# Cross-attention with a routed expert layer: scores of two heads at a time, one pair of banks ahead of the exponentials

## The chip, the cores and the metric

One NeuronCore of a Trainium2 chip runs the whole program in one launch. The metric is the device time of that launch in microseconds. The engines meant below are PE (TensorE), ACT (ScalarE), DVE (VectorE), POOL (GpSimd) and SP (SyncE, which here only issues DMAs).

## The reference

Eight batches of 112 tokens of width 512 attend to 375 context tokens each (257 image tokens and 118 text tokens, each part with its own key and value weights and its own softmax), with 16 heads of 32. Then each token goes through two of eight experts.

```python
x = x + xattn(layernorm(x), ctx)           # 8 x 112 x 512, ctx 8 x 375 x 512
#   q = rms_norm(x @ Wq.T + bq) * w ; k, k_img likewise from ctx_txt, ctx_img ; v, v_img linear
#   out = softmax(q k_img / sqrt(32)) v_img + softmax(q k / sqrt(32)) v   per head ; out @ Wo.T + bo
x = x + moe(layernorm(x))                  # gate softmax, top 2 of 8 experts,
#   expert: gelu(x W1 + b1) -> gelu(. W2 + b2) -> . W3 + b3
```

## The kernel before

All is float32 in and out. Products that need it are made of three fp32r products of high and low parts (high x high, high x low, low x high): the high part is a rounding copy on ACT, the low part a subtraction on DVE.

**Bodies and slots.** The attention part is a software pipeline written out in full: `body(b, p)` for b from -1 to 8 on each engine, each body with 16 slots `h`, one per head. In body b the heads of batch b are computed, the projections of batch b + 1 are prepared (`has_prep`, bodies -1 to 6), and the rest of batch b - 1 is done (`has_tail`: output projection, second LayerNorm, gate). Every engine goes through its own list in order, and the lists meet at semaphores, so the place of an instruction in its engine's list is the schedule.

**PE.** In slot h: every fourth slot (h = 0, 4, 8, 12) the scores of a group of four heads (`score`, L1042: 12 matmuls with 32 rows each, heads in different row groups, into the four PSUM banks of `scores`); then the transposes of the probabilities of head h - 2 (`transpose`, L1051, into `ptb`, `LAG` is 2); in slots 2, 6, 10, 14 the product with the values (`attend`, L1068 and L1072, into `pvb`); and a piece of projection work, the `FILL` of the slot: v2 in slots 0 and 1, k0 in 2, o (the output projection) in 3 and 4, xT in 4, k1 in 5, qt in 6 and 7, k2 in 8, q and kt in 9, kt in 10, kx and k3 in 11, v0 and ms in 12, v0 and rb in 13, v1 in 14 and 15. They use two PSUM banks (`tiles`) in turn, which ACT or DVE empties (`stage`).

**Softmax.** DVE's `maxima` (L753, L754) takes the negated maxima of two heads at a time for the image and the text part; ACT's `weigh` (L543, L545) makes the exponentials of one head with their sums, `take_transposed` (L553) copies the transposed probabilities. For a group of four heads, DVE's `invert_sums` (L761) writes reciprocals of the sums, each repeated 32 times, into `rx`; PE transposes them behind `attend`, ACT copies them (`take_sums`, L559), DVE multiplies (`attended`, L766, L768), and the result is split (L563, L772). DVE did both `maxima` of a group at the head of slots 0, 4, 8, 12; ACT did `weigh` ahead of `take_transposed` in the slots between, and at the end of those four slots.

**RMS norm.** The squares of q and k are written by ACT (`sq`: L499, L510, L519). DVE adds the four chunks (L833 in slot 11, L788 and L790 in slot 12), PE sums over partitions (`ms`, L1017), DVE scales (L736), POOL takes the power -0.5 (L442), PE spreads it (`rb`, L1021), ACT copies it (L516), and DVE multiplies queries and keys (L722, L700, L701). Then come the high and low parts of the next body's queries and first key chunk (L533, L526 on ACT, L747, L743 on DVE) in slot 14. The other key chunks are split in the slots of `KEYS_HIGH_AT` and `KEYS_LOW_AT`. ACT adds the bias to the image keys (L511) just behind their square.

**Context.** `cr` holds the raw context of a batch, loaded by SP (L308); ACT copies its image part in slot 0 and its text part in slot 2 (L280, `ch_done`), DVE subtracts in slots 1 and 3 (L672, `cl_done`). SP waits for both before the load of the next, and behind that load stand the load of x (L310), the store of `x1` (L334, after the bank of o is read), the store of `xn2` (L344) and the load of `xr` (L351). The last body's SP list begins with three loads of expert weights.

**After the attention** come routing on DVE and PE, the scatter by indirect DMAs, and a loop over blocks of 256 tokens with the expert weights (from about 460 us to the end); the change does not touch it.

Of the kernel before, what the change touches and what calls it, by code (L numbers as in the profile page):

```python
# [23 lines left out]
P = 128  # L24
# [38 lines left out]
KEYS_LOW_AT = {2: 1, 6: 2, 10: 3}  # L63
# [29 lines left out]
def cross_attention_moe(nc, x, ctxT, ctx_last, wT, vecs, o_b, wg, bg, experts, b12, b3, out):  # L93
    with ExitStack() as ctx:
# [41 lines left out]
        rx = sb("rx", [P, 2, 4, HD])  # L136
# [14 lines left out]
        for i in (1, 0):  # L151
# [87 lines left out]
            "x_in", "c_in", "ch_done", "cl_done", "xr_in", "xr_ob", "ln1_stats", "ln1_mv", "ln1_var", "ln1_rstd", "xn_done",  # L239
            "ln2_stats", "ln2_mv", "ln2_var", "ln2_rstd", "xh_done",  # L240
            "squares", "sum_a", "sum_b", "r_done", "rms_done", "q_done", "k_done", "qh_done", "ql_done", "kh_done", "kl_done", "rows_stored", "rows_in",
            "s_ready", "max_done", "exp_done", "rsum_done", "t_ready", "pt_done",
# [33 lines left out]
        def split_ctx(act, n, i):  # L276


            act.wait_ge(S["c_in"], 16 * n)
            act.activation(c_part(cH)[i], cr[:, :, PARTS[i]], ACT.Copy).then_inc(S["ch_done"], 1)  # L280

        @block.sync
        def _(sp):
# [12 lines left out]

            def body(b, p):
                if has_heads(b):

                    if b > 1:  # L300
                        sp.wait_ge(S["pv_ready"], NC * (b - 1))
                    sp.dma_start(vx[0:1, p, :], vlast_d[b:b + 1, :]).then_inc(vrow_in[p], 16)
                if has_prep(b):

                    if b < LAST - 1:
                        sp.wait_ge(S["ch_done"], 2 * (b + 2))
                        sp.wait_ge(S["cl_done"], 2 * (b + 2))
                        sp.dma_start(cr, ctxT[b + 2]).then_inc(S["c_in"], 16)  # L308
                        sp.wait_ge(S["xn_done"], b + 2)
                        sp.dma_start(xb[0:L, :], x[b + 2]).then_inc(S["x_in"], 16)  # L310
                if fixed(b, -1):

                    sp.wait_ge(S["zeroed"], 1)
                    by_partition = slots_d.rearrange("(p r) d -> p r d", p=P)
                    for r in range(0, ROWS, B):
                        n = min(B, ROWS - r)
                        sp.dma_start(by_partition[:, r:r + n, :], xr[:, :].unsqueeze(1).to_broadcast([P, n, D])).then_inc(S["zero_stored"], 16)

                    sp.wait_ge(S["vlast_sb"], 1)
                    sp.dma_start(vlast_d, vlast).then_inc(S["vlast_out"], 16)  # L320
                    sp.wait_ge(S["vlast_out"], 16)
                    sp.wait_ge(S["cleared"], 1)
                if fixed(b, LAST):


                    sp.wait_ge(S["pv_ready"], NC * LAST)
                    sp.wait_ge(S["cl_done"], 2 * B)
                    sp.wait_ge(S["k_done"], NC * B)
                    for pc in range(3):
                        sp.dma_start(raw[pc], experts[0, pc]).then_inc(raw_in[pc], 16)  # L330
                if has_tail(b):

                    taken(sp, "o", b)
                    sp.dma_start(x1_d[b - 1], x1[0:L, :]).then_inc(S["x1_stored"], 16)  # L334
                    if fixed(b, DONE):
# [78 lines left out]
        def _(pool):  # L414
# [55 lines left out]
        def _(act):  # L470
# [11 lines left out]
            def stage(name, b, p):  # L482
# [13 lines left out]
                if name == "q":  # L496

                    taken(act, "q", b)
                    act.activation(sq[:, :, 0:L], qn[:, 1 - p, :, :], ACT.Square).then_inc(S["squares"], 1)  # L499
# [5 lines left out]
                if name in ("k0", "k1", "k2", "k3"):  # L505

                    act.wait_ge(tile_ready[bank], cnt + 1)
                    c = int(name[1])
                    bias = vec[:, V_KIB, c:c + 1]
                    act.activation(sq[:, c, L:L + IMG], tiles[:, bank, 0:IMG], ACT.Square, bias=bias).then_inc(S["squares"], 1)  # L510
                    act.activation(kn[1 - p][:, c, 0:IMG], tiles[:, bank, 0:IMG], ACT.Identity, bias=bias).then_inc(tile_free[bank], 1)  # L511
# [5 lines left out]
                if name == "kx":  # L517
                    taken(act, "kx", b)
                    act.activation(sq[:, :, L + IMG:TOK], kn[1 - p][:, :, IMG:KEYS], ACT.Square).then_inc(S["squares"], 1)  # L519

            def split_keys(b, p, c):

                act.wait_ge(S["k_done"], NC * b + c + 1)
                if not (fixed(b, 0) and c < 2):
                    act.wait_ge(S["s_ready"], NC * b + c - 1)
                act.activation(kH[:, c % 2, :], kn[p][:, c, :], ACT.Copy).then_inc(S["kh_done"], 1)  # L526

            def split_queries(b, p):

                act.wait_ge(S["q_done"], b + 1)  # L530
                if not fixed(b, 0):
                    act.wait_ge(S["s_ready"], NC * b)
                act.activation(qH, qn[:, p, :, :], ACT.Copy).then_inc(S["qh_done"], 1)  # L533
# [36 lines left out]
            def body(b, p):  # L570
                for h in range(NH):
# [4 lines left out]
                    if h == 14 and has_prep(b):  # L576
                        split_queries(b + 1, 1 - p)
                        split_keys(b + 1, 1 - p, 0)
# [19 lines left out]
                    if h == 0 and has_prep(b) and not fixed(b, -1):  # L598
                        split_ctx(act, b + 2, 0)
                    for name in STAGE_AT[h]:  # L600
                        if has(name, b):
                            stage(name, b, p)
                    if h % 4 == 0 and has_heads(b):
                        weigh(b, p, h)
                    if h == 2 and has_prep(b) and not fixed(b, -1):
                        split_ctx(act, b + 2, 1)
# [48 lines left out]
        def _(dve):  # L655
# [14 lines left out]
            def split_ctx_low(n, i):  # L670
                dve.wait_ge(S["ch_done"], 2 * n - 1 + i)
# [77 lines left out]
            def maxima(b, g, i):  # L749

                dve.wait_ge(S["s_ready"], NC * b + g + 1)
# [4 lines left out]
            def invert_sums(b, g):  # L756
# [4 lines left out]
                dve.reciprocal(rx[0:L], sums[0:L, g % 2, :, :].unsqueeze(3).to_broadcast([L, 2, 4, HD])).then_inc(S["rsum_done"], 1)  # L761
# [16 lines left out]
            def body(b, p):  # L778
                for h in range(NH):
# [11 lines left out]
                    if h % 4 == 0 and has_heads(b):  # L791
                        maxima(b, h // 4, 0)
                        maxima(b, h // 4, 1)
# [16 lines left out]
                    if h in (1, 3) and has_prep(b) and not fixed(b, -1):  # L810
                        split_ctx_low(b + 2, h // 2)
# [35 lines left out]
                    if h == 0 and fixed(b, FIRST):  # L847
                        dve.wait_ge(S["small_in"], 64)

# [107 lines left out]
        def _(pe):  # L957
# [74 lines left out]
            def score(b, p, g):  # L1032
# [42 lines left out]
            def body(b, p):  # L1075
# [4 lines left out]
                for h in range(NH):  # L1080
                    if h % 4 == 0 and has_heads(b):
                        score(b, p, h // 4)
# [161 lines left out]
```

## Time and profile before

| | us |
|---|---|
| median of 3 runs | 931.02 (930.43 to 933.33) |
| the profiled execution | 931.23 |
| its span | 929.4 |
| attention bodies 1 to 6, each | 46.47 |

| engine | busy us | share of the span |
|---|---|---|
| PE (matmul) | 773.7 | 83% |
| PE (weight load) | 676.3 | 73% |
| DVE | 588.3 | 63% |
| ACT | 505.8 | 54% |
| POOL | 69.6 | 7% |

The shares are means over stages with different limits: set-up until 47 us, the attention bodies until about 415 us, routing and scatter until about 460 us, and then the experts. The ends of matmuls are modelled, so a busy PE is not one at its peak, and a gap between two matmuls is a little longer than the idle time that the profile gives. The time from one event to another is best taken start to start.

### The profile page before, as it was taken

How to read it: one execution, taken by the hardware profiler on the slowest of the kernel's cores; microseconds unless marked ns; L12 is line 12 of the kernel's file. 1: busy time of each engine (PE TensorE's matmuls, PEld its weight loads, DVE VectorE, ACT ScalarE, POOL GpSimd, SP SyncE). 2: the span in 40 equal slices, each digit the busy share in tenths (PEclk: the TensorE clock that was granted, in tenths of full speed). 3: DMA queues.
4: the chain of work that ended last, by engine and by line, in shares of the span. 5: the costliest groups of instructions: out<-in, count | busy, mean ns of one | idle time of the engine just before them, and what ended most of it. 6: DMA issues, size and time to landing. Idle time of an engine off the chain costs nothing.

```text
span 929.4 us, 17429 instructions
## 1 busy us (share of the span) xinstructions
PE 773.7 (83%) x6238; PEld 676.3 (73%) x6238; DVE 588.3 (63%) x1001; ACT 505.8 (54%) x1154; POOL 69.6 (7%) x94
## 2 busy tenths in 40 slices
PE   2888989898989898773079999999999999999930
PEld 2566666666666666552079999999999999999920
DVE  5466767676767676746136767676767676767634
ACT  4566767676767676751044545454545555555510
POOL 2100000000000000000600000000000000000014
PEclk9989999999999999855579999999999999999975
DMA  7850102010202000407625656565656565656568
GB/s 245 312 210 1 64 11 64 12 64 11 63 12 65 11 22 11 158 11 260 204 86 187 233 184 236 185 235 183 236 184 236 184 236 184 234 183 237 181 226 259
DMA packets 33982, 137.53 MB, mean 148 GB/s; under 512 B 3712, under 2 KB 3728, under 8 KB 22928
## 3 DMA queue, kind: packets, MB, share of 16 engines
q1 hardware_dynamic: 31200, 129.23, 40.0%
q0 software_dynamic: 2736, 7.69, 2.9%
q8 instruction: 28, 0.46, 0.2%
q14 instruction: 18, 0.15, 0.0%
HBM read 115.36 MB, written 21.54 MB: 147 GB/s over the span
## 4 chain that ended last, share of the span: by engine, by line
PE 68%; DVE 9%; ACT 9%; issue 7%; DMA 3%; POOL 2%; SPq 0%; POOLq 0%; ACTq 0%; DVEq 0%
PE tiles L960 7%; PE tiles L962 7%; PE tiles L961 7%; PE scores L1191 4%; PE scores L1193 4%; PE scores L1192 4%; PE ptb L1051 3%; PE pvb L962 3%; PE pvb L961 3%; PE pvb L960 3%; PE ptb L962 3%; PE ptb L961 3%; PE ptb L960 3%; PE scores L1042 2%; ACT scr L543 2%
## 5 line engine op out<-in xcount | busy, mean ns | idle before, releaser
L776 DVE TENSOR_TENSOR w<-scr,w 128x2048 fp32r<-128x2048 f32 x76 | 174.2, 2292 | 84.6 <-ACT w L568 84.6
L568 ACT ACTIVATE w<-scr 128x2048 fp32r<-128x2048 f32 x76 | 144.8, 1907 | 63.2 <-PE scores L1193 59.3
L960 PE MATMUL tiles<-c,w 128*128 128x256 f32 (+1 forms) x272 | 83.0, 305 | 22.1 <-DVE c L672 17.5
L1051 PE MATMUL ptb<-ident,scr 112*128 112x112 f32 x384 | 64.4, 279 | 25.9 <-ACT scr L553 25.9
L960 PE MATMUL tiles<-w 128*128 128x256 f32 x288 | 81.5, 283 | 0.0
L961 PE MATMUL tiles<-w 128*128 128x256 f32 x288 | 81.5, 283 | 0.0
L962 PE MATMUL tiles<-w 128*128 128x256 f32 x288 | 81.5, 283 | 0.0
L961 PE MATMUL tiles<-c,w 128*128 128x256 f32 (+1 forms) x272 | 79.9, 294 | 0.0
L962 PE MATMUL tiles<-c,w 128*128 128x256 f32 (+1 forms) x272 | 79.9, 294 | 0.0
L1051 PEld LDWEIGHTS ptb<-ident,scr 112*128 112x128 f32 x384 | 44.1, 149 | 48.9 <-ACT scr L545 35.1
L553 ACT ACTIVATE scr<-ptb 128x336 f32<-128x336 f32 x128 | 59.9, 468 | 26.9 <-PE ptb L1051 26.9
L960 PEld LDWEIGHTS tiles<-c,w 128*128 128x128 f32 x272 | 55.0, 202 | 25.4 <-issue 21.8
L543 ACT ACTIVATE scr<-scores,nmax 112x257 f32<-112x257 f32 x128 | 62.6, 489 | 12.7 <-DVE nmax L754 12.7
L933 DVE CAST w<-scr 128x256 fp32r<-128x256 f32 x144 | 41.6, 289 | 43.7 <-ACT scr L642 42.7
L935 DVE TENSOR_TENSOR w<-scr,w 128x256 fp32r<-128x256 f32 x144 | 61.2, 425 | 5.1 <-DVE w L933 0.2
L642 ACT ACTIVATE scr<-tiles,b12s 128x256 f32<-128x256 f32 x72 | 33.2, 473 | 56.9 <-PE tiles L962 56.8
L1191 PE MATMUL scores<-w 128*128 128x512 f32 x144 | 57.0, 396 | 0.0
L1193 PE MATMUL scores<-w 128*128 128x512 f32 x144 | 56.2, 390 | 0.0
L1192 PE MATMUL scores<-w 128*128 128x512 f32 x144 | 56.0, 389 | 0.0
L761 DVE RECIPROCAL rx<-sums 112x256 f32<-112x256 f32 x32 | 55.7, 1741 | 0.0
L961 PEld LDWEIGHTS tiles<-c,w 128*128 128x128 f32 x272 | 55.2, 203 | 0.4
L960 PEld LDWEIGHTS tiles<-w 128*128 128x128 f32 x288 | 55.3, 192 | 0.0
(212 smaller groups left out, 2120.9 us busy)
## 6 DMA issues: line engine op xcount, KB each, us to landing
scr<-in_dram SPq DMA_DIRECT2D x86, 1024.0 KB, 4.8
slots_d<-xr SPq DMA_DIRECT2D x3, 2048.0 KB, 17.5
scr<-in_dram SPq DMA_DIRECT2D x8, 750.0 KB, 4.9
scr<-slots_d SPq DMA_DIRECT2D x10, 512.0 KB, 4.6
slots_d<-scr SPq DMA_DIRECT2D x9, 512.0 KB, 3.8
xn<-in_dram SPq DMA_DIRECT2D x10, 256.0 KB, 4.7
xb<-in_dram SPq DMA_DIRECT2D x8, 224.0 KB, 4.9
xr<-in_dram SPq DMA_DIRECT2D x8, 224.0 KB, 2.5
```

The lines of the kernel that those rows point to most:

```text
L543: act.activation(probs[0:L, s, 0:IMG], scores[0:L, s, 0:IMG], ACT.Exp, bias=nmax[0:L, g, s, 0:1], accum_out=sums[0:L, g, 0, s:s + 1])
L553: act.activation(probT[:, h % 8, :, :], ptb[:, 0:KT * L].rearrange("p (t q) -> p t q", t=KT), ACT.Copy).then_inc(S["pt_done"], 1)
L568: act.activation(EH[slot], raw[slot], ACT.Copy).then_inc(S["eh_done"], 1)
L776: dve.tensor_tensor(EL[slot], raw[slot], EH[slot].bitcast(F32), ALU.subtract).then_inc(S["el_done"], 1)
L935: dve.tensor_tensor(hL[lay][:, c, :], gel[:, m % 4, :], hH[lay][:, c, :].bitcast(F32), ALU.subtract).then_inc(S["hl_done"], 1)
L960: pe.matmul(out, wh, xh, start=start, stop=False)
L961: pe.matmul(out, wh, xl, start=False, stop=False)
L962: return pe.matmul(out, wl, xh, start=False, stop=stop)
L1051: mm = pe.transpose(ptb[:, t * L:(t + 1) * L], probs[0:L, h % 4, t * P:(t + 1) * P], ident[0:L, 0:L])
L1191: pe.matmul(yb[:, t, :], h_hi, wh[:, i, :], start=(f == 0), stop=False)
L1192: pe.matmul(yb[:, t, :], h_hi, wl[:, i, :], start=False, stop=False)
L1193: mm = pe.matmul(yb[:, t, :], h_lo, wh[:, i, :], start=False, stop=(f == 7))
```

## The change

PE computes the scores of two heads at a time: `score(b, j)` for the pair j (heads 2j and 2j + 1), in two of the four banks, in the odd slots 2j - 1 behind the transposes; the first pair of a body is computed at the end of slot 15 of the body before. It waits for the exponentials of the heads up to 2j - 3, which the transposes ahead of it have waited for already. DVE takes the maxima of pair j at the end of slot 2j - 1 (pair 0 at the head of slot 0), and ACT's `weigh` stands ahead of `take_transposed` in every slot but slot 0, where it stands behind the split of the context; the splits for the next body's queries and first keys stand behind both in slot 14. `invert_sums` takes the reciprocals of the eight sums and then copies them 32-fold. All squares are made on POOL, from the keys and queries with their bias, and so is the copy of the text part of the context. The x1 store stands ahead of the context load on SP. Key chunk 3's low part moves from slot 10 to slot 9.

```diff
-KEYS_LOW_AT = {2: 1, 6: 2, 10: 3}
+KEYS_LOW_AT = {2: 1, 6: 2, 9: 3}
...
+            def next_context(b):
+                sp.wait_ge(S["ch0_done"], b + 2)
+                sp.wait_ge(S["ch1_done"], b + 2)
+                sp.wait_ge(S["cl_done"], 2 * (b + 2))
+                sp.dma_start(cr, ctxT[b + 2]).then_inc(S["c_in"], 16)
...
                     sp.dma_start(x1_d[b - 1], x1[0:L, :]).then_inc(S["x1_stored"], 16)
+                if FIRST <= b < LAST - 1:
+                    next_context(b)
...
+            def square(name, b, p):
+
+                taken(pool, name, b)
+                if name == "q":
+                    to, of = sq[:, :, 0:L], qn[:, 1 - p, :, :]
+                elif name == "kx":
+                    to, of = sq[:, :, L + IMG:TOK], kn[1 - p][:, :, IMG:KEYS]
+                else:
+                    c = int(name[1])
+                    to, of = sq[:, c, L:L + IMG], kn[1 - p][:, c, 0:IMG]
+                pool.tensor_tensor(to, of, of, ALU.mult).then_inc(S["squares"], 1)
...
                     rstd(b + 2, mv1, ve1, rs1, "ln1")
+                    if not fixed(b, -1):
+                        pool.wait_ge(S["c_in"], 16 * (b + 2))
+                        taken(pool, "v2", b)
+                        pool.tensor_copy(c_part(cH)[1], cr[:, :, PARTS[1]]).then_inc(S["ch1_done"], 1)
+                    if not fixed(b, -1):
+                        pool.wait_ge(tile_ready[tile_use("ms", b - 1)[0]], tile_use("ms", b - 1)[1] + 1)
+                    square("k0", b, p)
                 if has_tail(b):
                     rstd(b, mv2, ve2, rs2, "ln2")
                 if has_prep(b):
+                    for name in ("k1", "k2", "q", "kx", "k3"):
+                        square(name, b, p)
...
                     if fixed(b, -1) and h in WEIGHTS_AT:
                         split_weights(WEIGHTS_AT[h])
-                    if h % 4 and has_heads(b):
+                    if h and has_heads(b):
                         weigh(b, p, h)
                     if h < LAG:
                         if has_tail(b):
                             take_transposed(b - 1, NH - LAG + h)
                     elif has_heads(b):
                         take_transposed(b, h - LAG)
+                    if h == 14 and has_prep(b):
+                        split_queries(b + 1, 1 - p)
+                        split_keys(b + 1, 1 - p, 0)
...
-                dve.reciprocal(rx[0:L], sums[0:L, g % 2, :, :].unsqueeze(3).to_broadcast([L, 2, 4, HD])).then_inc(S["rsum_done"], 1)
+                dve.reciprocal(rsum[0:L], sums[0:L, g % 2, :, :]).then_inc(S["inverted"], 1)
+                dve.wait_ge(S["inverted"], NC * b + g + 1)
+                dve.tensor_copy(rx[0:L], rsum[0:L].unsqueeze(3).to_broadcast([L, 2, 4, HD])).then_inc(S["rsum_done"], 1)
...
+                    if h % 2 and h < NH - 1 and has_heads(b):
+                        maxima(b, (h + 1) // 2)
...
-                if not (fixed(b, 0) and g == 0):
-
-                    pe.wait_ge(S["exp_done"], NH * b + 4 * g)
+                if not (fixed(b, 0) and j < 2):
+
+                    pe.wait_ge(S["exp_done"], NH * b + 2 * j - 2)
                 for n, (q, k) in enumerate(((qH, kH), (qH, kL), (qL, kH))):
-                    for i in range(4):
+                    for i in (2 * j % 4, 2 * j % 4 + 1):
...
-                    if h % 4 == 0 and has_heads(b):
-                        score(b, p, h // 4)
...
+                    if h % 2 and h < NH - 1 and has_heads(b):
+                        score(b, (h + 1) // 2)
...
+                    if h == NH - 1 and has_prep(b):
+                        score(b + 1, 0)
```

## Rows read from the trace of the kernel before

**Rows 1.** The page: busy times, the chain that ended last, the context loads.

```profile
PE 773.7 (83%) x6238; PEld 676.3 (73%) x6238; DVE 588.3 (63%) x1001; ACT 505.8 (54%) x1154; POOL 69.6 (7%) x94
...
PE 68%; DVE 9%; ACT 9%; issue 7%; DMA 3%; POOL 2%; SPq 0%; POOLq 0%; ACTq 0%; DVEq 0%
...
scr<-in_dram SPq DMA_DIRECT2D x8, 750.0 KB, 4.9
```

**Rows 2.** Windows: stretch, its length, each engine's busy time, TensorE's clock, DMA.

```profile
185.47:231.94 46.47, 41.00 (x389) 31.92 (x388) 32.54 (x67) 33.09 (x113) 3.72 (x6) 1.00 0.12 38
...
387.60:412.00 24.40, 16.57 (x154) 12.27 (x154) 11.79 (x20) 12.46 (x48) 1.26 (x1) 0.50 0.07 20
```

**Rows 3.** TensorE's waits from 95 to 395 us: total us, times, longest.

```profile
PE ptb L1051 <- ACT scr L553: 20.5, 27, 1.9
PE tiles L1021 <- ACT scr L495: 4.1, 6, 0.7
PE scores L1042 <- ACT scr L545: 3.8, 6, 0.6
PE tiles L980 <- ACT xn L504: 2.9, 6, 0.5
PE tiles L960 <- DVE c L672: 2.8, 6, 0.5
PE tiles L960 <- DVE x L714: 2.0, 6, 0.3
```

**Rows 4.** Timeline of TensorE around a group's scores: start, length, instruction.

```profile
185.47 0.78 PE L1042 MATMUL scores<-kq 32*112 32x376 f32 x12
186.18 0.51 PE L1051 MATMUL ptb<-ident,scr 112*128 112x112 f32 x3
186.46 0.47 PE L1011 MATMUL tiles<-w,c 128*119 128x512 f32 x1
```

**Rows 5.** Timeline of slots 11 to 13: ACT, DVE and TensorE.

```profile
218.83 0.60 ACT L519 ACTIVATE scr<-scr 128x472 f32<-128x472 f32 x1 [0.90 <-DVE scr L738]
...
222.35 0.48 ACT L543 ACTIVATE scr<-scores,nmax 112x257 f32<-112x257 f32 x1 [1.23 <-DVE nmax L754]
...
220.74 0.67 DVE L790 TENSOR_TENSOR scr<-scr 128x487 f32<-128x487 f32 x1
221.33 0.68 DVE L753 TENSOR_REDUCE nmax<-scores 112x2 f32<-112x514 f32 x1
...
221.87 0.95 PE L1017 MATMUL tiles<-ones,scr 128*128 128x1 f32 x8
222.68 0.48 PE L1051 MATMUL ptb<-ident,scr 112*128 112x112 f32 x3
```

**Rows 6.** Timeline of slots 13 to 15: TensorE, DVE and ACT.

```profile
225.27 0.65 PE L1021 MATMUL tiles<-ident,rr 128*128 128x128 f32 x4 [0.69 <-ACT scr L495]
225.75 0.45 PE L1051 MATMUL ptb<-ident,scr 112*128 112x112 f32 x3
226.14 0.59 PE L1068 MATMUL pvb<-scr 128*32 128x112 f32 x16
...
230.12 0.48 PE L1051 MATMUL ptb<-ident,scr 112*128 112x112 f32 x3 [1.25 <-ACT scr L553]
...
228.28 0.63 DVE L747 TENSOR_TENSOR kq<-qn,kq 128x448 fp32r<-128x448 f32 x1
...
228.74 0.46 ACT L543 ACTIVATE scr<-scores,nmax 112x257 f32<-112x257 f32 x1
```

**Rows 7.** Groups of instructions: busy us, mean ns, idle before.

```profile
L761 DVE RECIPROCAL rx<-sums 112x256 f32<-112x256 f32 x32 | 55.7, 1741 | 0.0
...
L448 POOL TENSOR_TENSOR xr<-xr,obr 112x512 f32<-112x512 f32 x8 | 10.1, 1264 | 15.3 <-DMA xr<-in_dram 15.3
```

**Rows 8.** GpSimd's power (ns, min/median/max), and the timeline beside the first.

```profile
L442 POOL TENSOR_TENSOR rr<-msb,mhalf x8: 1017/1017/2997, 37.2 to 362.8; 128x4 f32<-128x4 f32 x8
...
37.04 2.28 DVE L686 TENSOR_TENSOR w<-scr,w 128x2048 fp32r<-128x2048 f32 x1
```

More of the change, by code:

```diff
@@ L135, in cross_attention_moe @@
         vx = sb("vx", [P, 2, D])
-        rx = sb("rx", [P, 2, 4, HD])
+        rsum, rx = sb("rsum", [P, 2, 4]), sb("rx", [P, 2, 4, HD])
         rbc, pvn, af = sb("rbc", [P, 2 * L]), sb("pvn", [P, 2 * L]), sb("af", [P, L])
@@ L238, in cross_attention_moe @@
             "vbias_done", "nq_done", "vlast_mm", "vlast_sb", "vlast_out",
-            "x_in", "c_in", "ch_done", "cl_done", "xr_in", "xr_ob", "ln1_stats", "ln1_mv", "ln1_var", "ln1_rstd", "xn_done",
+            "x_in", "c_in", "ch0_done", "ch1_done", "cl_done", "xr_in", "xr_ob", "ln1_stats", "ln1_mv", "ln1_var", "ln1_rstd", "xn_done",
             "ln2_stats", "ln2_mv", "ln2_var", "ln2_rstd", "xh_done",
             "squares", "sum_a", "sum_b", "r_done", "rms_done", "q_done", "k_done", "qh_done", "ql_done", "kh_done", "kl_done", "rows_stored", "rows_in",
-            "s_ready", "max_done", "exp_done", "rsum_done", "t_ready", "pt_done",
+            "s_ready", "max_done", "exp_done", "inverted", "rsum_done", "t_ready", "pt_done",
             "pv_ready", "rb_done", "pv_read", "a_done", "cleared", "ah_done", "al_done", "x1_stored",
@@ L279, in split_ctx @@
             act.wait_ge(S["c_in"], 16 * n)
-            act.activation(c_part(cH)[i], cr[:, :, PARTS[i]], ACT.Copy).then_inc(S["ch_done"], 1)
+            act.activation(c_part(cH)[i], cr[:, :, PARTS[i]], ACT.Copy).then_inc(S[("ch0_done", "ch1_done")[i]], 1)
         @block.sync
@@ L334, in body @@
                     sp.dma_start(x1_d[b - 1], x1[0:L, :]).then_inc(S["x1_stored"], 16)
+                if FIRST <= b < LAST - 1:
+                    next_context(b)
+                if has_tail(b):
                     if fixed(b, DONE):
@@ L495, in stage @@
                     act.activation(vn[p if t == 2 else 1 - p][0:rows, t, :], tiles[0:rows, bank, :], ACT.Copy).then_inc(tile_free[bank], 1)
-                if name == "q":
-                    taken(act, "q", b)
-                    act.activation(sq[:, :, 0:L], qn[:, 1 - p, :, :], ACT.Square).then_inc(S["squares"], 1)
                 if name in ("qt", "kt"):
@@ L509, in stage @@
                     bias = vec[:, V_KIB, c:c + 1]
-                    act.activation(sq[:, c, L:L + IMG], tiles[:, bank, 0:IMG], ACT.Square, bias=bias).then_inc(S["squares"], 1)
                     act.activation(kn[1 - p][:, c, 0:IMG], tiles[:, bank, 0:IMG], ACT.Identity, bias=bias).then_inc(tile_free[bank], 1)
@@ L516, in stage @@
                     act.activation(rms[:, :], tiles[:, bank, 0:TOK], ACT.Copy).then_inc(tile_free[bank], 1)
-                if name == "kx":
-                    taken(act, "kx", b)
-                    act.activation(sq[:, :, L + IMG:TOK], kn[1 - p][:, :, IMG:KEYS], ACT.Square).then_inc(S["squares"], 1)
             def split_keys(b, p, c):
@@ L524, in split_keys @@
                 if not (fixed(b, 0) and c < 2):
-                    act.wait_ge(S["s_ready"], NC * b + c - 1)
+                    act.wait_ge(S["s_ready"], 2 * (NC * b + c - 1))
                 act.activation(kH[:, c % 2, :], kn[p][:, c, :], ACT.Copy).then_inc(S["kh_done"], 1)
@@ L531, in split_queries @@
                 if not fixed(b, 0):
-                    act.wait_ge(S["s_ready"], NC * b)
+                    act.wait_ge(S["s_ready"], 2 * NC * b)
                 act.activation(qH, qn[:, p, :, :], ACT.Copy).then_inc(S["qh_done"], 1)
@@ L599, in body @@
                         split_ctx(act, b + 2, 0)
+                    if h == 0 and has_heads(b):
+                        weigh(b, p, h)
                     for name in STAGE_AT[h]:
@@ L670, in split_ctx_low @@
             def split_ctx_low(n, i):
-                dve.wait_ge(S["ch_done"], 2 * n - 1 + i)
+                dve.wait_ge(S[("ch0_done", "ch1_done")[i]], n)
                 dve.tensor_tensor(c_part(cL)[i], cr[:, :, PARTS[i]], c_part(cH)[i].bitcast(F32), ALU.subtract).then_inc(S["cl_done"], 1)
@@ L747, in split_queries_low, with maxima @@
                 dve.tensor_tensor(qL, qn[:, p, :, :], qH.bitcast(F32), ALU.subtract).then_inc(S["ql_done"], 1)
-            def maxima(b, g, i):
-                dve.wait_ge(S["s_ready"], NC * b + g + 1)
+            def maxima(b, j):
+                dve.wait_ge(S["s_ready"], 2 * NC * b + j + 1)
+                g, i = j // 2, j % 2
                 of = nmax[0:L, g % 2, 2 * i:2 * i + 2, :]
@@ L790, in body @@
                         dve.tensor_tensor(sq[:, 0, :], sq[:, 0, :], sq[:, 1, :], ALU.add).then_inc(S["sum_b"], 1)
-                    if h % 4 == 0 and has_heads(b):
-                        maxima(b, h // 4, 0)
-                        maxima(b, h // 4, 1)
+                    if h == 0 and has_heads(b):
+                        maxima(b, 0)
                     if h == 1 and has_tail(b):
@@ L809, in body @@
                         split_keys_low(b, p, KEYS_LOW_AT[h])
-                    if h in (1, 3) and has_prep(b) and not fixed(b, -1):
-                        split_ctx_low(b + 2, h // 2)
+                    if h in (1, 6) and has_prep(b) and not fixed(b, -1):
+                        split_ctx_low(b + 2, h // 5)
                     if h == 2 and has_tail(b):
@@ L1030, in stage, with score @@
                     mm.then_inc(tile_ready[bank], 1)
-            def score(b, p, g):
+            def score(b, j):
+                g = j // 2
                 pe.wait_ge(S["ql_done"], b + 1)
                 pe.wait_ge(S["kl_done"], NC * b + g + 1)
-                if not (fixed(b, 0) and g == 0):
-                    pe.wait_ge(S["exp_done"], NH * b + 4 * g)
+                if not (fixed(b, 0) and j < 2):
+                    pe.wait_ge(S["exp_done"], NH * b + 2 * j - 2)
                 for n, (q, k) in enumerate(((qH, kH), (qH, kL), (qL, kH))):
-                    for i in range(4):
+                    for i in (2 * j % 4, 2 * j % 4 + 1):
                         of = slice(HD * i, HD * i + HD)
@@ L1080, in body @@
                 for h in range(NH):
-                    if h % 4 == 0 and has_heads(b):
-                        score(b, p, h // 4)
                     if h < LAG:
```

10 lines of the change are left out of this document (1 added, 9 removed).

## The prediction

> **What bounds the kernel now.** I read the page's parts 1 and 4 first: GpSimd is idle and 68% of the chain that ended last is TensorE [rows 1]. The attention loop repeats with a period of 46.47 us in bodies 1 to 6, of which TensorE is busy 41.00 [rows 2]. So the next question is what the 5.47 us of idle time per body waits for. The list of TensorE's waits answers [rows 3]: over 300 us (6.46 bodies) 20.5 us go to a transpose waiting for ACT to empty `ptb` (27 times, four per body), 4.1 to `rb` waiting for the v0 copy, 3.8 to the scores waiting for the last exponential of the group before, 2.9 to `kx`, 2.8 and 2.0 to k0 and k1; together 36.1, 5.6 per body. None is TensorE's own; all are chains over ACT and DVE. So a saving on DVE or ACT is worth at most what it takes from these waits, and a microsecond added to TensorE counts unless it falls into one.
>
> **Scores.** One group (12 matmuls, four row groups side by side) takes from 185.47 to 186.18, 0.71 us, for three rounds of 376 columns [rows 4]. A pair has the same three rounds, two wide instead of four. Bounds for it: 0.35 (half, if issue set the time) and 0.71 (if the rounds do). The last LDWEIGHTS and matmuls come in rounds, all four at once, so I take 0.71. Place matters too: a full-height transpose is followed by a fill 0.28 later (186.18 to 186.46), but by a row-tiled product after 0.39 (225.75 to 226.14) [rows 4, 6]; a score behind a transpose therefore costs 0.71 + 0.15 = 0.86, and an old one behind a fill 0.71 + 0.10 = 0.81. Per body seven at 0.86 and one at 0.81 replace four at 0.81: 6.83 - 3.24 = 3.6 us more for TensorE.
>
> **Slots 0 to 10.** Here five new scores stand for two old ones: 5 x 0.86 - 2 x 0.81 = 2.68 more. What goes: the waits of scores, k0 and k1, and three of the four on `ptb` (their sizes in each body 0.44, 0.34 and 0.81). With 0.63, 0.49 and 0.33 that is 3.04 by the rows; start to start each is some 0.16 more, since ends are modelled: 4.0. The score's wait goes since `exp_done` of two heads back has been awaited by the transpose before it; k0's since the 1.74 us reciprocal [rows 7] becomes one over 8 numbers (at 6.8 ns each 0.05) and a copy of 256 columns (0.34 by the maxima's row, 514 columns in 0.68 [rows 5]); with the hand-over between them I take 0.5 (bounds 0.4 and 0.8), so DVE has 1.2 us x 4 less. What comes new: the exponentials of even heads now stand ahead of the copy of the transposed probabilities. In slot 4 that binds: LN's multiply in slot 3 waits for GpSimd, the maxima stand behind it (1.02 us from their start to the exponential, 221.33 to 222.35 [rows 5]), and from the exponential's start over the copy to the transpose it is 1.38 (228.74 to 230.12 [rows 6]); following both queues from the score at 0 this gives the transpose of slot 5 at 13.84 where TensorE is there at 12.86: 0.98. Slot 7's score waits 0.27 for the low half of key chunk 2, one slot nearer than before, slot 3's transpose 0.16. Sum: 2.68 - 4.0 + 1.41 = +0.1 us.
>
> **Slots 11 and 12.** Before [rows 5]: the square of kx on ACT (218.83, 0.60), three sums at once behind it until 221.41, then `ms` at 221.87, just when v0's half is done. Now the kx square runs on GpSimd. The only two-operand row there is 112x512 in 1264 ns [rows 7], 2.47 ns a column: 472 columns are 1.17 us, +0.57 (bounds: 0.60 as on ACT, 1.26 as the whole row). The first sum waits for it. Then, at the end of slot 11, DVE takes maxima (0.91 until the next instruction starts) before the sums of slot 12, where they used to be behind them. 221.41 + 0.57 + 0.91 = 222.89, and `ms` at 223.0 instead of 221.87: 1.13; slot 11's own start is 0.2 later by the score in front of kx. The second square, k3 (257 columns, 0.64), ends under these maxima. +1.3 us. The cover of the old chain was v0's half, and it is used up.
>
> **Slots 13 to 15.** Score 7 lies between the transpose at 222.68 and v0's second half, and `rb` behind that waits for the v0 copy as before: +0.86, all of it on the path. Then before [rows 6]: `rb` 225.27, DVE through normalising at 228.28, ACT's exponential at 228.74 behind two splits, the copy, the transpose of slot 15 at 230.12 after 1.25 idle. Now DVE does maxima 7 at 228.28, and the exponential waits for them: 229.30, +0.56. The splits move behind it, but end at about the transpose + 1.0, before the score at transpose + 1.8. +1.4 us.
>
> **Sum.** 0.1 + 1.3 + 1.4 = 2.8 us per body, period 49.3. Seven bodies (0 to 6): +20. Body -1: `ms` 0.7 later (GpSimd squares), the first score now ahead of the last value row's products and the copy behind them: +1.2 together. Last body: no k, no squares; three old group bubbles go, while the x1 store still lands behind the three experts' loads: +0.6, within ±4. Span 929.4 + 21.8 = 951.2; the profiled run lies 1.8 above its span (931.23, 0.2 above the median of 931.02): **953 us**.
>
> **At nothing.** ACT loses six squares and one context copy; it idles in front of the maxima anyway (1.23 before 222.35 [rows 5]), and gives nothing to a chain that waits for DVE. The context copy on GpSimd is needed by slot 9 and is there in slot 3. On SP the x1 store is put ahead of the context load, which is now issued in slot 6 or 7 instead of 4; its 4.9 us [rows 1] have 8 slots of 2.8 us before they are read; the xn2 store and the xr load are queued behind it, and their waits (slots 7 and 11) end later than the load's. Without that cover a late load would hold up ACT's split in slot 0.
>
> **GpSimd beside VectorE.** Seven of eight powers on GpSimd took 1017 ns, the first 2997 [rows 8]; it began at 37.20 beside a DVE subtraction of two SBUF operands (37.04 to 39.32) and ended 0.88 after that one's end. So such pairs run one after the other. The Trainium skill ("SBUF — State Buffer", Who interferes with whom) says this of a VectorE instruction with two SBUF inputs against a GpSimd one that reads SBUF: whichever is first holds the pair for its whole length. By that rule, the trace agrees. What it does here, by the rows: the k3 square starts on GpSimd the moment kx's is done, and the first sum, released by the same event, has to wait 0.64 for it: +0.6 per body, 7 x 0.64 = 4.5, 957.5 us. I keep it as a rival, since DVE may win the race, and then nothing is lost.
>
> **Rivals.** (a) The forecast, new chains longer than TensorE's work: 0.55. (b) The same with the serial GpSimd and DVE above, 957 to 962: 0.18. For: the 2997 ns row; against: it needs the race. (c) Other side: TensorE alone sets the end. If the maxima fall into DVE's idle time, TensorE has 3.6 more work and loses 4.0 + 0.7 of waiting (slots 0 to 11), keeping 0.88 and 1.43 before `rb` and slot 15: -1.1 x 7 = -8, 923 us; with pairs at 0.5 instead of 0.71 another 8 x 0.21 x 7 = 12 less, 911. It decides at slot 12: it holds if `ms` isn't later than v0's half. For it: DVE is busy 32.5 of 46.5 us and loses 5. Against: the sums and maxima there stand in one queue. 0.17. (d) Gains and new waits cancel, for instance squares at ACT's speed and rounds half as long: 931, 0.10. A lower clock I rule out: body 7 fell to half clock (387.6 to 412, PE busy 68% [rows 2]) while a body at full clock is busy 88%, and the new one 43.8 / 49.3 = 89%.
>
> **Range and chances.** 926 to 966: the low end leaves out most of (c), the high end adds 0.64 x 7 and 1 us per body for pitches I misjudged. (a)'s own range is 943 to 960. 0.3% is 2.8 us, about what can be told from no change. Faster 0.17, same 0.08, slower 0.75 ((a), (b) and a part of (d)).
>
> **What would show it.** Score starts 49 us apart instead of 46.5; pair scores of 0.7 us; a TensorE gap of about 2 us before `ms` (released by the sum) and one of about 2 before slot 15's transpose; k0, k1 and kx without waits; reciprocals under 0.3. If `ms` has no gap, (c) is right. If GpSimd's square of k3 and the first sum never overlap, (b).

## The result and the profile after

The changed kernel takes 967.5 us (median of 4, 962.2 to 970.6) against 931.2 (median of 4): ratio 1.038, 95% interval 1.0327 to 1.0434. Slower, as forecast, but by 36 us where 22 were forecast, and above the range's end of 966. The changed kernel's own runs also scatter over 8 us, those of before over 3; the last section comes back to this.

The first lines of the page after, to be held against [rows 1]: busy times, TensorE's granted clock in 40 slices, and the chain that ended last.

```profile
PE 819.0 (85%) x6238; PEld 708.0 (73%) x6238; DVE 559.2 (58%) x1033; ACT 483.8 (50%) x1099; POOL 109.8 (11%) x149
...
PEclk9998989999898979975558999999999999999975
...
PE 72%; DVE 10%; issue 6%; ACT 5%; DMA 3%; POOL 3%; SPq 0%; POOLq 0%; ACTq 0%; DVEq 0%
```

DVE, ACT and GpSimd changed as meant (29 and 22 us less, 40 more). TensorE is busy 45 us longer with the same 6238 matmuls, and among the nines of the clock in the attention bodies there now stand eights and a seven, about one per body. So the next view is a window per body, from one body's first score to the next's, with the busy times, the clock and the DMA columns of [rows 2].

```profile
46.04:100.04 54.00, 45.78 (x337) 33.51 (x337) 27.65 (x61) 29.57 (x102) 7.82 (x11) 0.91 0.26 94
100.04:150.61 50.57, 46.38 (x390) 35.84 (x389) 28.88 (x71) 30.25 (x107) 8.90 (x13) 0.93 0.11 35
150.61:200.59 49.98, 46.42 (x389) 35.88 (x388) 28.86 (x71) 30.25 (x107) 8.90 (x13) 0.93 0.12 35
200.59:252.37 51.78, 47.89 (x389) 36.97 (x388) 28.85 (x71) 30.24 (x107) 8.89 (x13) 0.90 0.11 34
...
304.23:358.41 54.18, 49.73 (x389) 38.30 (x388) 29.52 (x71) 30.33 (x107) 8.57 (x13) 0.87 0.11 32
358.41:407.40 48.99, 43.63 (x389) 33.88 (x389) 28.89 (x71) 30.25 (x107) 8.91 (x13) 1.00 0.05 16
407.40:967.40 560.00, 469.07 (x3455) 438.19 (x3454) 334.14 (x518) 253.78 (x341) 34.85 (x37) 0.89 0.57 197
...
238.70:248.90 10.20, 9.51 (x62) 6.96 (x62) 3.05 (x12) 1.64 (x4) 2.26 (x2) 0.50 0.01 2
```

The difference of the spans, 38.0 us, lies in bodies 0 to 6: 361.4 us against 324.1, +37.2. All before them gives 1.2 back, all behind them adds 1.9. The only body that kept its full clock took 48.99 us (49.3 were forecast, 46.47 before); the others 50.0 to 54.2, each with a stretch of 3.4 to 10.2 us at the lower of the two levels, 1.2 GHz, such as the last row's 10.2 us. Most of these stretches begin behind `ms`, ahead of which TensorE now stands idle; one in body 0 and one in body 5 (320.6 to 324.0) begin near slot 5. Body 0 of the kernel before has 6.8 us at the lower level, too.

The waits of TensorE, 95 to 395 us, against [rows 3]:

```profile
PE ptb L1075 <- ACT scr L574: 11.0, 11, 1.8
PE tiles L1040 <- DVE scr L812: 9.4, 5, 1.9
PE tiles L1044 <- ACT scr L524: 3.4, 5, 0.7
```

As forecast the waits of the scores, of kx, k0 and k1 are gone, and there is a new one of 1.9 us ahead of `ms` (now L1040). Here are slots 11 and 12, the answer to [rows 5]; the instructions of DVE, GpSimd and ACT, then TensorE:

```profile
232.93 0.64 DVE L757 TENSOR_TENSOR scr<-tiles,vec 128x472 f32<-128x472 f32 x1
234.66 1.06 DVE L854 TENSOR_TENSOR scr<-scr 128x487 f32<-128x487 f32 x1 [1.09 <-POOL scr L452]
235.64 0.68 DVE L773 TENSOR_REDUCE nmax<-scores 112x2 f32<-112x514 f32 x1
236.55 0.65 DVE L810 TENSOR_TENSOR scr<-scr 128x487 f32<-128x487 f32 x1
237.24 0.67 DVE L812 TENSOR_TENSOR scr<-scr 128x487 f32<-128x487 f32 x1
...
233.65 1.55 POOL L452 TENSOR_TENSOR scr<-scr 128x472 f32<-128x472 f32 x2 [5.56 <-DVE scr L757]
...
236.67 0.48 ACT L564 ACTIVATE scr<-scores,nmax 112x257 f32<-112x257 f32 x1 [2.41 <-DVE nmax L774]
...
238.05 1.26 PE L1040 MATMUL tiles<-ones,scr 128*128 128x1 f32 x8 [1.87 <-DVE scr L812]
239.18 0.80 PE L1075 MATMUL ptb<-ident,scr 112*128 112x112 f32 x3
```

The maxima (L773) stand between the first and the second sum, and the gap is there: 1.87 us, where about 2 was forecast. From the score that opens this body (200.59) to the transpose behind `ms` it is 38.59 us, where the same place before is 37.21 (185.47 to 222.68). From there on the clock is low: the three transposes last 0.80 instead of 0.48, and from slot 13's transpose to slot 14's it is 6.46 us (239.18 to 245.64), where the body that kept its clock needs 3.96 (396.76 to 400.72). That body shows slot 15, against [rows 6] (TensorE, ACT, DVE):

```profile
400.23 0.65 PE L1044 MATMUL tiles<-ident,rr 128*128 128x128 f32 x4 [0.69 <-ACT scr L524]
...
405.59 0.48 PE L1075 MATMUL ptb<-ident,scr 112*128 112x112 f32 x3 [1.75 <-ACT scr L574]
...
404.19 0.48 ACT L564 ACTIVATE scr<-scores,nmax 112x257 f32<-112x257 f32 x1 [2.70 <-DVE nmax L774]
...
403.17 0.68 DVE L773 TENSOR_REDUCE nmax<-scores 112x2 f32<-112x514 f32 x1
```

From `rb` to the transpose of slot 15 it is 5.36 us; before it was 4.85.

### The profile page after: what moved, and what is told of

Read it like the earlier page. It is cut to its first block, busy times and chain, and to the rows that moved or that the text cites. A ratio compares the mean times of both kernels' runs of the same rounds, so it can differ in the third digit from the quotient of the medians.

```text
span 967.4 us, 17507 instructions
## 1 busy us (share of the span) xinstructions
PE 819.0 (85%) x6238; PEld 708.0 (73%) x6238; DVE 559.2 (58%) x1033; ACT 483.8 (50%) x1099; POOL 109.8 (11%) x149
## 4 chain that ended last, share of the span: by engine, by line
PE 72%; DVE 10%; issue 6%; ACT 5%; DMA 3%; POOL 3%; SPq 0%; POOLq 0%; ACTq 0%; DVEq 0%
PE tiles L983 7%; PE tiles L985 7%; PE tiles L984 7%; PE scores L1066 4%; PE ptb L1075 4%; PE scores L1217 3%; PE scores L1219 3%; PE scores L1218 3%; PE ptb L983 3%; PE ptb L985 3%; PE ptb L984 3%; PE pvb L985 3%; PE pvb L984 3%; PE pvb L983 3%; PE pvb L1092 3%
## 5 line engine op out<-in xcount | busy, mean ns | idle before, releaser
L983 PE MATMUL tiles<-c,w 128*128 128x256 f32 (+1 forms) x272 | 82.8, 304 | 15.2 <-DVE c L691 12.6
L1075 PEld LDWEIGHTS ptb<-ident,scr 112*128 112x128 f32 x384 | 49.1, 157 | 38.3 <-ACT scr L566 26.2
L983 PEld LDWEIGHTS tiles<-c,w 128*128 128x128 f32 x272 | 54.7, 201 | 18.0 <-issue 17.6
L956 DVE CAST w<-scr 128x256 fp32r<-128x256 f32 x144 | 41.6, 289 | 44.4 <-ACT scr L661 43.4
L494 POOL DMA_INDIRECT scr<-slots_d,slotu x16 | 15.6, 972 | 444.6 <-SPq L408 440.0
L983 PEld LDWEIGHTS tiles<-w 128*128 128x128 f32 x288 | 55.3, 192 | 0.0
L984 PEld LDWEIGHTS tiles<-w 128*128 128x128 f32 x288 | 55.3, 192 | 0.0
## 6 DMA issues: line engine op xcount, KB each, us to landing
slots_d<-xr SPq DMA_DIRECT2D x3, 2048.0 KB, 16.8
```

The lines of the kernel that those rows point to most:

```text
L983: pe.matmul(out, wh, xh, start=start, stop=False)
L984: pe.matmul(out, wh, xl, start=False, stop=False)
L1075: mm = pe.transpose(ptb[:, t * L:(t + 1) * L], probs[0:L, h % 4, t * P:(t + 1) * P], ident[0:L, 0:L])
```

## The experiments

Each experiment tests a theory against a rival, as its expectation says. Theory A at the start: the changed order makes new chains (some 20 us), and the idle time in them brings the low clock (the rest). Kernels e1 to e4 and e9 are edits of the changed kernel; ratios are to the kernel before, run beside them on the same chip. Where a diff shows only the lines that matter, "..." stands for the rest.

**e1: throw-away matmuls in the gap ahead of `ms`.** Nothing else differs, and they end 0.2 us ahead of the sum.

```diff
                 elif name == "ms":
+                    for r in range(7):
+                        pe.matmul(tile[:, :], wv(WQ)[0][:, 0, 0:P], wv(WQ)[0][:, 1, :], start=True, stop=True)
                     pe.wait_ge(S["sum_b"], n + 1)
```

> The changed kernel with seven throw-away matmuls (512 columns, about 1.6 us at full clock) put into TensorE's gap ahead of ms, in every body; they are overwritten by ms. They cost nothing if the gap of 1.87 us stays. Theory A (the low clock of 6.8 to 10.2 us behind ms is brought on by the idle time of the slots, so of the 36 us some 17 are clock): no half-clock stretch between 100 and 400 us, every body 49 us like the one that kept its clock, total about 950. Rival B (the clock falls for another reason, such as row groups used two wide, or it would fall whatever stands in the gap): the stretches stay, total 967.

951.7 us (1.024, 1.0218 to 1.0262). The windows of bodies 1 and 2 to 6:

```profile
97.78:146.75 48.97, 45.29 (x397) 35.23 (x396) 28.92 (x71) 30.26 (x107) 8.91 (x13) 1.00 0.12 36
146.75:391.43 244.68, 226.39 (x1978) 176.11 (x1977) 144.50 (x351) 151.28 (x531) 44.58 (x65) 1.00 0.11 32
```

Work added, nothing taken away, and 16 us less: in bodies 1 to 6 the clock is 1.00 and each takes 48.9 to 49.0. This is shown: without the idle stretch ahead of `ms` these bodies have no low clock, and the low clock costs 16 us. The other two gaps, 0.95 us ahead of slot 5's transpose and 1.77 ahead of slot 15's, are still there at full clock. Bodies 0 to 6 take 344.6 us, 20.4 more than before; of the 37.2 in the changed kernel 16.8 are clock.

**e2: maxima of pair 6 behind the sums.**

```diff
+                    if h == 12 and has_heads(b):
+                        maxima(b, 6)
...
-                    if h % 2 and h < NH - 1 and has_heads(b):
+                    if h % 2 and h < NH - 1 and h != 11 and has_heads(b):
                         maxima(b, (h + 1) // 2)
```

> The changed kernel with the maxima of pair 6 moved on VectorE from the end of slot 11 to behind the sums of squares of slot 12. Theory A (maxima between the sums are 0.91 us of the gap ahead of ms): gap 1.87 to 0.95, 0.9 us a body at full clock (6 us), and with a shorter gap fewer half-clock stretches, total 948 to 961. Rival (the exponentials of heads 12 and 13, now 1.3 us later, hold up TensorE in slots 13 and 14 instead): ms in time, but as much lost behind it, total 965 to 970.

969.0 us (1.0424, 1.0402 to 1.0447), no gain. The rival holds:

```profile
PE ptb L1077 <- ACT scr L574: 17.7, 18, 1.8
PE tiles L1042 <- DVE scr L812: 5.8, 6, 1.0
```

The gap ahead of `ms` fell from 1.87 to 0.96, but the transpose of slot 13 now waits 1.17 for its copy, since ACT's copy stands behind an exponential that waits for the later maxima. The 0.9 us were on two chains. The low clock is in all of bodies 0 to 6, although the gap ahead of `ms` is half as long.

**e3: squares back on ACT** (the lines that the change removed from `stage`, L499, L510, L519 of before).

```diff
-                    square("k0", b, p)
...
-                    for name in ("k1", "k2", "q", "kx", "k3"):
-                        square(name, b, p)
...
+                    act.activation(sq[:, c, L:L + IMG], tiles[:, bank, 0:IMG], ACT.Square, bias=bias).then_inc(S["squares"], 1)
...
```

> The changed kernel with all six squares of a body back on ScalarE (the context copy stays on GpSimd). Theory A (kx's square is 0.97 us on GpSimd against 0.60, and the first sum, 1.06 instead of 0.66 us, waits for GpSimd's k3 square): gap ahead of ms 1.87 to about 1.1, 0.8 us a body, total 950 to 962. Rival (ScalarE needs the relief of 3 us a body): exponentials and copies come later elsewhere, total 967 or more.

954.9 us (1.0255, 1.0223 to 1.0287): 12.6 less than the changed kernel, and the gap ahead of `ms` is 1.05. Still every one of bodies 0 to 6 but the last shows the low clock. Here are bodies 1 to 6:

```profile
94.50:399.28 304.78, 283.19 (x2329) 218.47 (x2328) 169.13 (x421) 195.55 (x673) 25.56 (x42) 0.92 0.11 31
```

That is 21.6 us of idle time in six bodies, 3.6 each, where the kernel before has 5.47 each at full clock. So idle time alone doesn't tell the clock, and theory A had a hole.

**e4: maxima of pair 7 ahead of the normalising.**

```diff
                         invert_sums(b, (h - 5) // 4)
+                    if h == 13 and has_heads(b):
+                        maxima(b, 7)
...
-                    if h % 2 and h < NH - 1 and has_heads(b):
+                    if h % 2 and h < NH - 1 and h != 13 and has_heads(b):
                         maxima(b, (h + 1) // 2)
```

> The changed kernel with the maxima of pair 7 moved on VectorE from behind slot 13's normalising (which waits for rb) to ahead of it. Theory A (the chain rb, copy, normalising, maxima, exponential, copy sets the transpose of slot 15, 1.75 us late at full clock): that gap goes to under 0.7, 1 us or more a body (7 to 9 us), total 952 to 960. Rival (the score that follows then waits for the splits, or the gap ahead of ms grows): total 965 to 968.

963.8 us (1.036, 1.0339 to 1.0382), 3.8 less than the changed kernel, which is no more than that kernel's own scatter. The gap itself went as theory A had it: in body 4, at full clock again from 293.0 on, slot 15's transpose starts without a wait, and the waits of up to 1.1 us for the copy that are left are all in slot 5.

```profile
250.46:299.14 48.68, 45.01 (x389) 34.91 (x388) 29.21 (x71) 30.29 (x106) 8.56 (x13) 0.96 0.12 36
...
297.34 0.45 PE L1077 MATMUL ptb<-ident,scr 112*128 112x112 f32 x3
```

The gain expected from it (7 to 9 us) didn't come, because the low-clock stretches behind the gap of 1.87 ahead of `ms` stayed and were no shorter: 51 us in bodies 1 to 6, for 44 in the changed kernel.

**e9: copy ahead of the exponential in even slots.**

```diff
-                    if h and has_heads(b):
+                    if h % 2 and has_heads(b):
                         weigh(b, p, h)
...
                         take_transposed(b, h - LAG)
+                    if h and h % 2 == 0 and has_heads(b):
+                        weigh(b, p, h)
```

> The changed kernel with ScalarE's copy of the transposed probabilities put back ahead of the exponentials in the even slots (as the kernel before had it in every fourth). Theory A (the transposes of slots 5 and 15 wait for a copy that stands behind exponentials that wait for maxima; 0.96 and 1.76 us a body at full clock): both gaps under 0.2, period at full clock 48.9 to about 46.5, the gap ahead of ms stays at 1.87, total 938 to 952 by how often the clock falls. Rival (the exponentials are late themselves, and the transposes two slots on wait as long): total 960 or more.

955.3 us (1.0264, 1.0229 to 1.0299), above the expected 938 to 952. The waits for the copy are gone altogether, which shows where they came from; but `ms` keeps its 1.87, and the first score of a body now waits up to 1.28 for the splits, which stand behind the exponential in slot 14:

```profile
PE tiles L1042 <- DVE scr L814: 11.2, 6, 1.9
PE scores L1068 <- DVE kq L768: 5.1, 4, 1.3
```

**e10: e2, e3 and e9 together.**

> The changed kernel with three of its orders undone: squares on ScalarE, the maxima of pair 6 behind the sums, copies ahead of exponentials in even slots; pair scores, small reciprocals and the context copy on GpSimd stay. Theory A (all new gaps come from these three; what is left is TensorE's own work, 3 us more than before, and 0.7 ahead of rb): no gap over 0.7, full clock through bodies 1 to 6, period 45.5 to 47.0, total 924 to 935. Rival (pairs ahead cost by themselves, through TensorE's mode or clock): period over 48, total over 945.

928.0 us (0.9955, 0.9941 to 0.997). Body period 45.9, clock 1.00 over bodies 1 to 6, although the first score of each body waits 1.27 for the splits as in e9:

```profile
93.70:369.16 275.46, 260.37 (x2328) 203.62 (x2329) 168.62 (x421) 195.54 (x673) 25.67 (x42) 1.00 0.12 35
```

With the three orders undone, the rest of the change no longer loses against the kernel before. Together they are worth 40 us; one by one it was 13 (e3), 12 (e9) and -1 (e2).

**e7: small reciprocals alone in the kernel before** (the `reciprocal` and `tensor_copy` of the change's `invert_sums`).

> The kernel before with the small reciprocals alone (8 numbers, then a copy of 256 columns). Theory A (VectorE's reciprocals of 1.74 us stand in the way of k0's context part, 0.49 a body, and of copies behind slot 8, 0.81): 0.5 to 1.3 us a body less, total 922 to 928, clock full. Rival (VectorE idles behind each of them anyway): 929 to 932.

926.0 us (0.9931, 0.9914 to 0.9948), as expected. The body takes 45.8 instead of 46.47: k0's wait went, the four waits for the copy stayed. This one part of the change gains 6 us by itself, more than all that e10 gains.

**e11: a gap in the old schedule.** A reduction on VectorE that nobody reads delays the sums.

```diff
...
+                        dve.tensor_reduce(idle[:, :], ones[:, :].unsqueeze(1).to_broadcast([P, 14, P]), AX.X, ALU.max)
                         dve.wait_ge(S["squares"], (NC + 2) * (b + 2))
```

> The kernel before, with a throw-away reduction of about 1.9 us on VectorE ahead of the sums of squares in slot 12 of bodies -1 to 6, so that ms comes about 1.5 us late. It asks what a gap of TensorE alone does in the old schedule, with its scores of four heads. Theory A (it is idle time that brings the low clock): half-clock stretches in most bodies behind ms, period 46.47 + 1.5 + 2 or more, total 950 to 960. Rival B (it takes the pairs or another part of the change): full clock, period about 48, total 941 to 944.

947.7 us (1.0174, 1.0148 to 1.02), between the two expectations. Of the 15.5 us, 5.5 lie ahead of the first score, in body -1 (52.74 for 47.21). The gap is 1.44 us, and the clock stays full in five of bodies 0 to 6, with periods of 48.1 to 48.2. Bodies 1 to 6, one of them with a stretch of 6.8 us at the lower level:

```profile
98.74:389.06 290.32, 250.15 (x2329) 193.08 (x2329) 206.75 (x403) 198.70 (x678) 22.36 (x36) 0.99 0.11 33
```

That speaks against theory A as it stood.

**e14: the same gap in e10's schedule** (the same line with 10 rows for 14). **e17: the old schedule with 18 rows.** Theory C, new here, is that the gap lowers the clock only with the pair scores beside it.

> The kernel of e10 (pair scores, its new gaps undone, full clock, period 45.9) with a throw-away reduction of 1.3 us on VectorE ahead of the sums of slot 12, to make the gap ahead of ms about 1.4 us, as in e11, where the old schedule kept its full clock in five of six bodies. Theory C (idle time ahead of ms is not enough by itself; the pair scores beside it, with six narrow matmuls in slots 11 and 13, make the difference): half-clock stretches in most bodies, total over 945. Theory A (the gap alone decides): as in e11, mostly full clock, period 47.2, total 937 to 942.

> The kernel before with a throw-away reduction of about 2.5 us on VectorE ahead of the sums of slot 12: a gap ahead of ms of about 2.0 us, as in the changed kernel (1.87), with the old scores of four heads. Theory A (size of the gap decides): half clock behind ms in most bodies, period over 50, total 960 or more. Theory C (it takes the pairs beside the gap): period 48.8 and full clock in most bodies, total 948 to 953.

e14 took 956.5 us (1.0269, 1.0251 to 1.0286), e17 954.1 (1.0249, 1.0226 to 1.0272). Bodies 1 to 6 of e14 and of e17:

```profile
97.60:394.29 296.69, 278.33 (x2330) 216.45 (x2329) 176.71 (x427) 196.02 (x674) 25.63 (x42) 0.93 0.11 32
```

```profile
98.28:392.85 294.57, 252.51 (x2330) 195.08 (x2329) 210.14 (x403) 198.39 (x678) 22.31 (x36) 0.98 0.10 32
```

With a gap of 1.54 in front of `ms`, e14 has a low-clock stretch in each of bodies 0 to 6 (3.4 to 10.2 us); e17 with 1.98 in three of seven, e11 with 1.44 in two. One execution of each was profiled, but the clock over the whole launch, which is known for every run, says the same: 0.901 to 0.906 in e14's four, 0.912 to 0.927 in e17's, 0.923 to 0.928 in e11's. A longer gap in the old schedule lowers the clock less often than a shorter one in e10's, so the gap's size isn't what decides between the two; whether it counts at all, two bodies against three don't show. What decides is the schedule around the gap: with the pair scores the clock falls where it mostly holds with groups of four. That is as theory C expected, but what in it does this (two row groups at a time, or where the scores stand: in slots 11 and 13 on either side of the gap, instead of slot 12) stays open. It may also be another part of e10's schedule, such as the order of the copies or the context copy on GpSimd; no run separates these. The throw-away reduction of 1.48 us cost 28 us in e14, while one of 2.01 us cost 15.5 in e11.

**e15: the kernel before with small reciprocals, and slot 14's splits behind exponential and copy.**

```diff
-                    if h == 14 and has_prep(b):
-                        split_queries(b + 1, 1 - p)
-                        split_keys(b + 1, 1 - p, 0)
...
                         take_transposed(b, h - LAG)
+                    if h == 14 and has_prep(b):
+                        split_queries(b + 1, 1 - p)
+                        split_keys(b + 1, 1 - p, 0)
```

> The kernel before with two parts of the change alone: the small reciprocals, and the splits of slot 14 behind that slot's exponential and copy (the maxima of those heads are long there, as all four are taken in slot 12). Theory A: the gap of 1.25 us ahead of slot 15's transpose goes, the splits end no later since they wait for the normalising: period 45.8 to 44.6, total 916 to 920. Rival (the exponential and copy delay the splits and the next body's scores by as much): 925.

917.4 us (0.9839, 0.9823 to 0.9856), as expected, the fastest of all, 14.7 below the kernel before on the same chip. The body takes 44.33 us:

```profile
182.12:226.44 44.32, 40.60 (x390) 31.96 (x389) 27.82 (x71) 33.15 (x113) 3.73 (x6) 1.00 0.13 40
```

**e16: e10 with slot 14's splits between copy and exponential.**

```diff
                         take_transposed(b, h - LAG)
-                    if h and h % 2 == 0 and has_heads(b):
-                        weigh(b, p, h)
                     if h == 14 and has_prep(b):
                         split_queries(b + 1, 1 - p)
                         split_keys(b + 1, 1 - p, 0)
+                    if h and h % 2 == 0 and has_heads(b):
+                        weigh(b, p, h)
```

> The kernel of e10 with ScalarE's splits of slot 14 between the copy and the exponential of that slot, since its scores wait 1.26 us for them at the end of slot 15. Theory A: that gap goes, period 45.9 to 44.7, total 917 to 922, so pairs ahead end where e15 does and gain nothing beside it. Rival (the exponential of head 14, now later, holds up the transpose at the head of the next body): period 45.5 or more, total 925 or more.

922.9 us (0.9915, 0.9887 to 0.9942), body 45.0, both between the two expectations and nearer to theory A. Bodies 1 to 6, of e16 and of e15:

```profile
89.62:359.71 270.09, 260.16 (x2330) 203.95 (x2329) 168.02 (x421) 196.81 (x673) 25.61 (x42) 1.00 0.12 35
```

```profile
93.46:359.41 265.95, 243.59 (x2329) 191.75 (x2328) 166.91 (x421) 198.94 (x678) 22.34 (x36) 1.00 0.11 36
```

TensorE is idle 1.7 us a body in e16 (9.93 / 6) and 3.7 in e15, and yet e15's body is 0.7 us shorter: the pairs ahead do remove the waits, but TensorE is busy 43.4 us a body instead of 40.6, which is more than the waits were.

## Why the prediction was right in its direction and wrong in its size

- **Pair scores at 0.71, 0.86 behind a transpose: right.** In the changed kernel a pair starts at 203.42 and the next fill at 204.12. TensorE's busy time in a body at full clock rose from 41.00 to 43.63.
- **Slots 0 to 10, +0.1: right within half a microsecond.** In the body at full clock it is 30.00 us to slot 11's transpose (358.41 to 388.41), before 30.35: -0.35. The wait at slot 5 came, 0.96 for 0.98; those of k0, k1, `kx` and the scores went. The small wait of slot 7's score was 0.08, 0.15 start to start, not 0.27. Reciprocal and copy took 0.19 and 0.29, 0.5 with the hand-over, as taken.
- **Slots 11 and 12, +1.3: right, with two errors that partly cancel.** Transpose to transpose 8.35 us (388.41 to 396.76) for 6.86: +1.5. GpSimd's square of kx took 0.97, not 1.17; the first sum took 1.06 instead of 0.67, because the k3 square had started 0.08 us before it:

```profile
L854 DVE TENSOR_TENSOR scr<-scr x8: 668/1061/1064, 34.6 to 392.5; 128x487 f32<-128x487 f32 x8
```

  So rival (b) was real, but cost 0.39 where 0.64 was priced: the sum ended 0.52 after the square (235.20 to 235.72), so most of its 0.67 was done behind it. The Trainium skill ("SBUF — State Buffer", Who interferes with whom) has the later one fully blocked; these numbers agree with that, apart from 0.15 us. Body -1 shows the other order: there the sum starts first (34.63) and lasts its 0.67, and the square behind it (34.90) takes 0.87 instead of 0.62. It ends 0.47 after the sum, so again 0.14 less than its whole length; what these 0.14 to 0.15 us are is not shown.
- **Slots 13 to 15, +1.4: right.** From slot 13's transpose to slot 15's 8.83 us for 7.44: +1.4. Of it 0.51 is `rb` to slot 15 (0.56 worked out), and the rest is score 7. The three sum up to +2.5 a body; e1's bodies 1 to 6 took 293.7 us for 278.7, the same 2.5, where 2.8 was forecast.
- **Bodies -1 and 0, +4.0 together: undersized by 1.2.** The first score came earlier (46.04), since the last value row's products moved behind it and so into body 0; e1 ended body 0 at 97.78, before 92.62: +5.2. The last body and all behind it: +1.9 for 0.6 in the changed kernel, -0.1 in e1.
- **"A lower clock I rule out": this is the step that failed.** It compared shares of busy time of whole bodies (89% for 88%) with the last body's 68%. The share came as worked out (43.63 of 48.99 us in the body that kept its clock, 89%), and the clock fell in six of seven bodies all the same. The kernel before had a warning in its own body 0, at 84% (38.17 of 45.41) and 0.92:

```profile
47.21:92.62 45.41, 38.17 (x325) 30.03 (x326) 29.11 (x60) 30.78 (x107) 2.98 (x4) 0.92 0.28 101
```

  Some 16 of the 36 us are this: e1, which only fills the gap, takes 951.7 us, 1.3 from the 953 that the other terms gave, and its bodies 0 to 6 are 20.4 longer than before where +20 was forecast. The range had no room for it: its high end holds rival (b) and 1 us a body for pitches (together 964.5, not 966), and nothing for the clock. The share over a body hides a stretch in which the gate and `ms` (products of 8 columns and of 1), a gap of 1.9 us and a pair of scores lie close together. Which of them the low clock needs beside the gap was not tried, so that part of its cause stays open.

Rival (c), that the maxima would fit into idle time, fell at the place named for it, slot 12. e10 and e16 show what it would have taken, other orders on DVE and ACT: e10 comes to 928.0, and only with the splits moved as well does e16 reach the 923 of this rival (922.9).

## What to carry to other kernels

Before an order is changed, follow each queue through a whole period with start-to-start times of the trace: it gave the large new gaps here to 0.3 us. Then look where the new gap falls: here it brought TensorE's low clock for three to ten microseconds, so that a gap of 1.9 us cost 2.4 more a body (16.8 over seven), which a mean over the period doesn't show; filling it with throw-away matmuls tests this in one run. A copy that frees a buffer belongs ahead of work that waits for something new in the same queue, and one move is not enough to see what an order is worth, since two chains may hold the same slot.

## What the runs showed of the hardware beside this

- The level of the clock is not told by idle time: e3's bodies 1 to 6 have 21.6 us of it with the clock at 0.92, e17's 42.1 (294.57 - 252.51) at 0.98, those of the kernel before 32.7 (278.72 - 246.05) at 1.00.
- The changed kernel's scatter goes with its clock: 970.6 and 969.5 us at a mean of 0.903 and 0.907, 965.6 and 962.2 at 0.917 and 0.918. But scatter alone is no sign of the low clock: e4, with low-clock stretches in every body, scatters over 1.6 us, and e16, at full clock in all of them, over 5.2.
- GpSimd's elementwise product with one tensor as both operands: 617 ns for 257 columns, 973 for 472, 936 for 448, so 1.66 ns a column and about 0.19 fixed, where the sum of two different tensors takes 1264 to 1280 for 512. (The operation differs, too; no run tells which of the two it is.)
